# A state-space block and a mixture of experts on one core: the low parts of the expert weights move from GpSimd to VectorE

## The reference

```
x  = x + layernorm(scan(layernorm(x)))          # selective state-space scan, 16 states
xt = layernorm(x)                               # T x 512
p  = softmax(xt @ gate_w)                       # 8 experts
for k in 0, 1:                                  # the two best experts of a token
    e, w  = k-th best expert and its probability
    pos   = place of the token among those of its expert
    keep  = pos < 640
    h = gelu(xt @ w1[e] + b1[e]);  y = h @ w2[e] + b2[e] + gelu(xt @ wd[e]) @ wu[e]
    out += keep * w * y
out += 0.2 * (gelu(xt @ sw1 + sb1) @ sw2 + sb2 + gelu(xt @ swd) @ swu)     # shared expert
x  = x + layernorm(out)
```

## Time and profile before

| what | value |
|---|---|
| median of three runs | 3465.41 us (3461.23 to 3466.05) |
| profiled execution: time, span | 3467.13 us, 3465.4 us |
| granted TensorE clock, mean | 0.937 |
| busy: PE, DVE, ACT, POOL | 3129.6, 1893.0, 1418.3, 1764.3 us |
| the same as share of the span | 90%, 55%, 41%, 51% |

### The profile page before, as it was taken

The page is one execution under the profiler, slowest core; times in us unless marked ns, Lnnn a source line. Parts: engine busy times, 40 slices in busy tenths (PEclk is TensorE's granted clock), DMA queues, the critical chain, the costliest instruction groups (busy, mean ns, idle before and its releaser), DMA issues.

```text
span 3465.4 us, 42917 instructions
## 1 busy us (share of the span) xinstructions
PE 3129.6 (90%) x15139; PEld 2558.2 (74%) x15139; DVE 1893.0 (55%) x2592; ACT 1418.3 (41%) x2514; POOL 1764.3 (51%) x1655
## 2 busy tenths in 40 slices
PE   6455698989989999899999999999999999999997
PEld 3233477777767777788888888888888888888886
DVE  6698899898988994562232232232322322322456
ACT  7554576766767665321221321322312213213233
POOL 1086888888878795551441541523513414416324
PEclk8655799999999999999999999999999999999999
DMA  7859597786968865930330320412312303304355
GB/s 253 253 174 229 183 242 194 222 235 191 270 183 235 218 199 187 282 92 19 76 77 13 98 62 15 119 35 49 98 22 68 82 16 92 67 10 109 72 179 164
DMA packets 277800, 466.31 MB, mean 135 GB/s; under 512 B 31073, under 2 KB 106545, under 8 KB 277586
## 3 DMA queue, kind: packets, MB, share of 16 engines
q1 hardware_dynamic: 209104, 273.30, 27.4%
q0 software_dynamic: 66720, 189.87, 20.9%
q10 hardware_dynamic: 1762, 0.40, 0.1%
HBM read 366.33 MB, written 97.16 MB: 134 GB/s over the span
## 4 chain that ended last, share of the span: by engine, by line
PE 52%; DVE 2%; DMA 1%; issue 1%; ACTq 1%; ACT 1%; SPq 0%; POOL 0%; POOLq 0%; DVEq 0%
PE c_psH L1953 26%; PE c_psY L1997 25%; DMA out<-d_y 1%; PE c_psT L1944 1%; ACTq L48 1%; DVE hh L1685 1%; DVE yst L1669 1%; PE c_psY L1993 0%; DVE hl L1687 0%; ACT h L1415 0%; ACT h L1417 0%; PE c_psT L2052 0%; DVE hl L1680 0%; DVE wgt L1847 0%; DVE hh L1679 0%
## 5 line engine op out<-in xcount | busy, mean ns | idle before, releaser
L1685 DVE CAST hh<-h 128x512 fp32r<-128x512 f32 (+1 forms) x400 | 213.3, 533 | 1155.1 <-ACT h L1417 1148.3
L1417 ACT ACTIVATE h<-c_psH,biases 128x512 f32<-128x512 f32 (+1 forms) x400 | 248.1, 620 | 1257.4 <-PE c_psH L1953 1192.3
L837 POOL TENSOR_TENSOR u<-dtxs,Bt 128x512 f32<-128x512 f32 x512 | 669.1, 1342 | 166.4 <-DVE b_psA L739 143.9
L739 DVE TENSOR_TENSOR_SCAN b_psA<-b_psA,b_few,u 128x512 f32<-128x512 f32 x512 | 656.8, 1283 | 63.1 <-ACT b_psA L607 61.5
L1997 PE MATMUL c_psY<-W2h,hh 128*128 128x512 f32 x1344 | 540.3, 402 | 28.6 <-issue 14.7
L954 PE MATMUL b_psY<-ident,pr 128*128 128x128 f32 x2048 | 348.1, 309 | 213.4 <-DVE pr L746 195.3
L1997 PE MATMUL c_psY<-W2l,hh 128*128 128x512 f32 x1344 | 528.8, 393 | 0.0
L1997 PE MATMUL c_psY<-W2h,hl 128*128 128x512 f32 x1344 | 527.6, 393 | 0.0
L1492 POOL DMA_INDIRECT xrow<-xt_d,slot_lists x80 | 91.1, 1139 | 812.1 <-PE c_psT L1944 429.8
L954 PEld LDWEIGHTS b_psY<-ident,pr 128*128 128x128 f32 x2048 | 266.5, 157 | 298.6 <-DVE pr L746 246.4
L746 DVE TENSOR_TENSOR pr<-b_psA,Ct 128x512 f32<-128x512 f32 x512 | 354.3, 692 | 20.6 <-DMA Ct<-bc_d 3.0
(11 more groups left out here) (267 smaller groups left out, 5737.2 us busy)
## 6 DMA issues: line engine op xcount, KB each, us to landing
w<-ws_d POOLq DMA_DIRECT2D x224, 512.0 KB, 6.6
raw<-in_w SPq DMA_DIRECT2D x256, 256.0 KB, 2.7
Bt<-bc_d SPq DMA_DIRECT2D x64, 512.0 KB, 17.4
Ct<-bc_d SPq DMA_DIRECT2D x64, 512.0 KB, 19.6
xn<-in_x SPq DMA_DIRECT2D x8, 1024.0 KB, 6.3
xT_d<-xnT SPq DMA_DIRECT2D x8, 1024.0 KB, 8.4
dt_d<-a_dt SPq DMA_DIRECT2D x8, 1024.0 KB, 7.0
dtx_d<-a_dx SPq DMA_DIRECT2D x8, 1024.0 KB, 7.3
```

Source lines behind the costliest of these rows:

```text
L739: nc.vector.tensor_tensor_scan(psA[q][:, :], psA[q][:, :], u[g % U_RING][:, :], carry[:, k:k + 1], ALU.mult, ALU.add).then_inc(s_h, 1)
L837: nc.gpsimd.tensor_tensor(u[g % U_RING][:, :], dtx[s % 2][:, :], Bt[n // TG][:, n % TG, :], ALU.mult)\
L1417: nc.scalar.activation(h32[:, 0:n * P], psH[j % 2][:, 0:n * P], ACT.Gelu, bias=b1[:, j - 1:j]).then_inc(s_gelu, 1)
L1685: nc.vector.tensor_copy(hh[j % 2][a], h32[a]).then_inc(s_hhi, 1)
```

## The change

Five edits:

1. `lows` moves from GpSimd's queue to VectorE's. VectorE's `run` gets the arguments `wset` and `rest` that ScalarE's already has: in a third block, and in the shared block, it makes the low parts of chunk j - 2 after chunk j, and those of chunks 15 and 16 at chunks 1 and 3 of a first block. GpSimd keeps its DMAs alone.
2. In the shared block the one-hot rows are weighed by token number on ScalarE (64 multiplications by a per-partition scale) and no more on VectorE (8 large ones). ScalarE's extra steps come after its conversions, and the weights of the router are stored at chunk 7, not 8.
3. The logits are turned into the two PSUM banks of the row transposes (`psT`) and no more into the banks of the down products (`psY`), in two halves, one after the other. VectorE copies them out after chunk 0's hidden tile (8 copies, not 4), and TensorE's `down(0)` no more waits for that copy.
4. The biases are turned into one bank, with one semaphore step.
5. In the last block of `mix`, TensorE signals each of the four output tiles when it is done, and VectorE scales them one by one.

```diff
@@ mix @@
+        s_tile = sem("b_last_tiles")
             def shared_out(b, t):
-                dve.wait_ge(s_mm2, (b + 1) * J)
+                if b < FB - 1:
+                    dve.wait_ge(s_mm2, (b + 1) * J)
+                else:
+                    dve.wait_ge(s_tile, t + 1)
...
+                        if b == FB - 1 and j == FC and t < BT - 1:
+                            last.then_inc(s_tile, 1)
-                last.then_inc(s_mm2, 1)
+                last.then_inc(s_tile if b == FB - 1 and j == FC else s_mm2, 1)
@@ experts @@
+        def logits_out(b):
+            return psT[b % 2][:, :, :].rearrange("p a b -> p (a b)")
+        def logit_column(b):
+            return 2 * P + (b % 4 // 2 * 2 + b // 4) * BT * E
@@ scalar @@
                     if wset is not None and j >= TRAIL:
                         convert_chunk(wset, j - TRAIL, at)
                     if rest is not None and j in REST_AT:
                         convert_chunk(rest[0], J - TRAIL + REST_AT.index(j), rest[1])
+                    if extra and j in extra:
+                        for part in extra[j]:
+                            part()
...
+            def weigh_one_hots(i):
+                act.wait_ge(s_heq, i + 1)
+                for o in range(BATCH):
+                    t = i * BATCH % NT + o
+                    high = high1[:, i % 2, o, :]
+                    last = nc.scalar.mul(high, high.bitcast(F32), tok_f[:, t:t + 1])
+                last.then_inc(s_high, 1)
@@ gpsimd @@
-            for j in range(J - 6):
-                lows(1, j)
             slots_known(0)
             gathers(0, 0, range(2))
             pool.wait_ge(s_wst, K * 16)
             gather_weights(0, 0)
-            for j in range(J - 6, J - TRAIL):
-                lows(1, j)
             gathers(0, 1, range(2))
             store_shared(SB - 1)
-            for j in range(J - TRAIL, J):
-                lows(1, j)
...
                 scatter(e, 1)
-                for j in range(J - TRAIL):
-                    lows(e + 2, j)
                 gathers(e + 1, 1, range(2))
                 scatter(e, 2)
-                for j in range(J - TRAIL, J):
-                    lows(e + 2, j)
                 gathers(e + 1, 1, range(2, 4))
@@ vector @@
+            def lows(s, j):
+                for w_ in pieces_of(j):
+                    _, _, hi, lo, view = piece(SHARED_W, w_)
+                    if w_ in (2, 3):
+                        hi, view = lo, view[0:LR, :]
+                    dve.wait_ge(s_whi, first_piece(s) + w_ + 1)
+                    nc.vector.tensor_tensor(lo, view, hi.bitcast(F32), ALU.subtract).then_inc(s_wlo, 1)
-            def run(at, nxt=None, extra=None, late=None, leaves=True, front=FRONT):
+            def run(at, nxt=None, wset=None, rest=None, extra=None, late=None, leaves=True, front=FRONT):
...
+                    if wset is not None and j >= TRAIL:
+                        lows(wset, j - TRAIL)
+                    if rest is not None and j in REST_AT:
+                        lows(rest, J - TRAIL + REST_AT.index(j))
...
-                dve.wait_ge(s_heq, i + 1)
-                v.tensor_tensor(high, high.bitcast(F32), spread(tok_f[:, r], E * ST), ALU.mult).then_inc(s_high, 1)
...
-            routing = {0: [less_max], 1: [probabilities, lambda: pick(0), lambda: mark(0)],
+            routing = {0: [logits, less_max], 1: [probabilities, lambda: pick(0), lambda: mark(0)],
-            run(shared(SB - 1), nxt=(expert(0, 0), X_OF[0]), front=FRONT_0, extra=routing)
+            run(shared(SB - 1), nxt=(expert(0, 0), X_OF[0]), front=FRONT_0, wset=1, extra=routing)
@@ tensor @@
                     if j == 0:
-                        if lead:
-                            pe.wait_ge(s_lg, 4)
...
             def turn_logits():
                 pe.wait_ge(s_lin, SB * 16)
+                pe.wait_ge(s_b1, 2)
+                for half in range(2):
+                    after(pe, s_lT, half)
...
```

More of the change, by code:

```diff
@@ L1420, in run @@
                         x_hi(*nxt, front.index(j - 1))
-                    if extra and j in extra:
-                        for part in extra[j]:
-                            part()
                     if weigh and j in WEIGH_AT and WEIGH_AT.index(j) < n:
@@ L1450, in store_weights @@
                         .then_inc(s_wst, 16)
-            run(shared(SB - 1), b1T[:, E * FC:], nxt=(expert(0, 0), X_OF[0], None), front=FRONT_0, wset=1, extra={1: (exponentials,), 8: (store_weights,)})
+            def weigh_one_hots(i):
[5 more added lines that the diff above has]
+                last.then_inc(s_high, 1)
+            steps = {1: [exponentials], 7: [store_weights]}
+            for i, j in enumerate(BATCH_AT):
+                steps.setdefault(j, []).append(lambda i=i: weigh_one_hots(i))
+            run(shared(SB - 1), b1T[:, E * FC:], nxt=(expert(0, 0), X_OF[0], None), front=FRONT_0, wset=1, extra=steps)
             def expert_blocks(e, last=False):
@@ L1479, in _ @@
         def _(pool):
-            def lows(s, j):
-                for w_ in pieces_of(j):
-                    _, _, hi, lo, view = piece(SHARED_W, w_)
-                    if w_ in (2, 3):
-                        hi, view = lo, view[0:LR, :]
-                    pool.wait_ge(s_whi, first_piece(s) + w_ + 1)
-                    nc.gpsimd.tensor_tensor(lo, view, hi.bitcast(F32), ALU.subtract).then_inc(s_wlo, 1)
             def gather(e, k, t):
@@ L1916, in first_block @@
             def first_block(e):
-                run(expert(e, 0), late=expert(e - 1, 2), nxt=(expert(e, 1), X_OF[1]), extra={12: (lambda: scatter_rows(e),)})
+                run(expert(e, 0), late=expert(e - 1, 2), nxt=(expert(e, 1), X_OF[1]), rest=e + 1,
+                    extra={12: (lambda: scatter_rows(e),)})
             for e in range(E - 1):
@@ L1922, in _ @@
                 expert_slots(e + 1)
-                run(expert(e, 2), late=expert(e, 1), nxt=(expert(e + 1, 0), X_OF[0]))
+                run(expert(e, 2), late=expert(e, 1), nxt=(expert(e + 1, 0), X_OF[0]), wset=e + 2)
             e = E - 1
@@ L2018, in turn_biases @@
                 pe.wait_ge(s_bin, 32)
-                nc.tensor.transpose(psT[0][:, 0, :], raw[0][:, 0:P], ident[:, :]).then_inc(s_bt, 1)
-                nc.tensor.transpose(psT[1][:, 0, 0:FC], raw[1][0:FC, 0:P], ident[0:FC, 0:FC]).then_inc(s_bt, 1)
+                nc.tensor.transpose(psT[0][:, 0, :], raw[0][:, 0:P], ident[:, :])
+                nc.tensor.transpose(psT[0][:, 1, 0:FC], raw[1][0:FC, 0:P], ident[0:FC, 0:FC]).then_inc(s_bt, 1)
             def turn_logits():
                 pe.wait_ge(s_lin, SB * 16)
-                for t in range(NT):
-                    b = t // BT
-                    k, o = b % 4 * 32, (b // 4 * BT + t % BT) * E
-                    last = nc.tensor.transpose(psY[b % 4][:, o:o + E], logits_in(b)[:, t % BT * P:(t % BT + 1) * P],
-                                               ident[k:k + E, k:k + E])
-                last.then_inc(s_lT, 1)
+                pe.wait_ge(s_b1, 2)
+                for half in range(2):
+                    after(pe, s_lT, half)
+                    for t in range(NT):
+                        b, o = t // BT, logit_column(t // BT) + t % BT * E
+                        if b % 4 // 2 == half:
+                            k = b % 4 * 32
+                            last = nc.tensor.transpose(logits_out(b)[:, o:o + E],
+                                                       logits_in(b)[:, t % BT * P:(t % BT + 1) * P], ident[k:k + E, k:k + E])
+                    last.then_inc(s_lT, 1)
             def cumulate():
```

19 lines of the change are left out of this document (9 added, 10 removed).

## The result

The kernel after takes 3419.96 us in the median of four runs (3419.75 to 3425.09), the kernel before 3465.73 beside it; the ratio is 0.9874 [0.9857, 0.9892]. Forecast were 3419 us, within 3411 to 3434. The profiled execution took 3419.83 us, its span is 3418.1. The mean granted clock rose from 0.937 to 0.944. In a second round, where the kernel after ran again as `after_again`, it took 3427.98 us beside 3469.14, a ratio of 0.9879 [0.9863, 0.9896]: 41.2 us and not 45.8. The change is worth 41 to 46 us, and the forecast's 46.2 was met at the upper end.

The account below looks back on a forecast made before the run. GpSimd's subtractions were taken to hold VectorE's copies and so TensorE, whose clock then drops. Gains of 34.9 + 6.5 + 3.0 + 1.8 = 46.2 us off the profiled 3467.13 gave 3420.9, or 3419.2 for a median; range 3411 to 3434.

Parts of the forecast that it names:

- First blocks: First blocks of experts 1 to 7: without GpSimd's subtractions VectorE's copy is no longer held; gain 34.9 us, bounds 33.2 to 36.6.
- The 1.7 us kept for `hl` at chunk 1: First blocks: half of the remaining 3.4 us of TensorE's waits for a low part, taken as staying; bounds 0 and 3.4.
- rival B: First blocks, chunk 3: VectorE's own queue keeps the stall; 3454 us, or 3433 for a part of it; chance 0.06 together.
- Second and third blocks: Low parts on VectorE in third blocks hide behind TensorE, and second and third blocks show no loss to remove; 0 us.
- rival D: Third blocks: VectorE's queue, waiting for raw weights, becomes the bound and the kernel gets slower; chance 0.04.
- no wait: Third blocks: a sign of being right was that ScalarE no longer waits for raw weights, 28.3 us in 7 waits before.
- Shared block, late: Late stall of TensorE in the shared block: 4.15 us of wait and 2.3 of slow clock both go; 6.5 us.
- Shared block, early: Start of the shared block: earlier first down product and clock lead by 5.1 us, of which 3.0 stay; bounds 0 and 5.1.
- I take another 0.6 off: Shared block, chunks past 4: allowance for ScalarE's one-hot multiplications and a full VectorE, cutting the lead from 3.6 to 3.0 us.
- End of `mix`: Last block of mix: scaling tile by tile puts three of four output tiles ahead of the last matmul; 1.8 us, or 0.
- rival A: Shared block: the early lead is 0 and up to 10 us more go in chunks 4 to 9; 3422 to 3432; chance 0.14.
- Rival C: First blocks: VectorE's subtractions hold GpSimd's scatters, the last ending 2.8 us later, so ScalarE waits; 3439 us; chance 0.05.

Follow-up runs that it names:

- pauses: Kernel before, but GpSimd waits for its own last subtraction to end before starting the next; 3436.52 us, ratio 0.9907.
- last_four_back: Kernel after, but the four subtractions of chunks 15 and 16 return to GpSimd behind its scatters, for experts 1 to 7; 3455.83 us, ratio 0.9958.
- three_more_steps: Kernel after with shared-block chunk 0's low parts before second pick, one-hots weighed on VectorE, third scatter held until next block's chunk 0 is split; 3424.07 us.
- low_parts_longer: Kernel after with two needless statistics operations on VectorE ahead of each main-weight subtraction, from expert 1's third block on; 3433.54 us, ratio 0.9893.
- logits_back: Kernel after with the logits again turned into the down products' banks, so the first down product waits for their copy; 3421.19 us, ratio 0.9885.
- weigh_on_vector: Kernel after with the one-hot rows weighed on VectorE again, none on ScalarE; 3418.37 us, ratio 0.9874.
- low_first: Kernel after with chunk 0's low parts in the shared block made ahead of the second pick and mark; 3420.52 us, ratio 0.988.
- pairs_back: Kernel after with the last four output tiles of mix scaled only after the last matmul again; 3423.24 us, ratio 0.9889.
- two_input: Kernel before with the hidden tile's high part made as its maximum with itself, a two-input operation, instead of a copy; 3478.47 us, ratio 1.0023.
- only_lows: Kernel before with only the move of the low parts from GpSimd to VectorE; 3429.26 us, ratio 0.9885.

## Why the prediction was right

**First blocks (34.9 forecast, 34.9 measured).** `pauses` and `last_four_back` show the cause. The 1.7 us kept for `hl` at chunk 1 were right in size and not in place: the wait that stays, 0.24 us a block above expert 0's (50.08 against 49.84), is at `down(0)`, behind VectorE's small copy, which takes 0.60 us beside a scatter. In `three_more_steps` the scatter is held back, and the blocks take 49.75 to 49.78 us (one takes 50.11). The subtractions at chunks 1 and 3 of a first block cost nothing, as the count of 2.8 us of work in 2.8 said; rival B did not come.

**Second and third blocks (0 forecast, 0.6 us lost).** The third blocks have no wait of TensorE. The 0.6 is mostly one pair of blocks, expert 3's, with 185.62 us where the others take 185.15. That is above the 185.5 which the prediction named as a sign of rival D, but it is not D: the time goes in the second block, where VectorE makes no weight. Its `down(0)` comes 0.35 us late. There a scatter began just ahead of VectorE's small copies, the first of which started 0.35 us later and the second took 0.64 us. In before the copy began 0.13 us ahead of the scatter, the copies took 0.42, and the scatter 1.74 instead of 1.57. ScalarE's waits for raw weights did not go but shrank, from 28.3 us and 2.0 (W1 and W2) to 10.6 and 6.8, none over 2.0:

```profile
ACT W1h L1380 <- DMA raw<-in_w: 10.6, 8, 1.5
ACT W2h L1380 <- DMA raw<-in_w: 6.8, 7, 2.0
```

That the loads come sooner with a quicker low part was right; "no wait" was too strong. Rival D was as far off as it looked: `low_parts_longer` nearly fills VectorE and loses nothing in these blocks.

**Shared block, late (6.5 forecast, 6.5 measured).** From `down(7)` to `down(14)` TensorE leads over before by 1.6 us throughout; at the end of the block it is 8.1, and the wait of 4.15 us is gone.

**Shared block, early (3.0 forecast, 1.6 measured in this trace).** This term was mis-sized, and 1.6 is the best that it shows. At `down(14)`, ahead of the late stall, the five traces of this same block lead over before by 1.6, 1.2, -0.8, -0.8 and -1.5 us (a minus is a lag); three are below the lower bound of 0. Its first half was right in direction: `down(0)` came 2.27 us earlier (2.3), and with the clock at 1.00 the lead at `down(1)` was 4.8 (5.1), though other traces have 1.1 to 2.2 and 3.7 to 4.7; `logits_back` gives back 2.7 us of wait and the clock of 0.60.

Of this lead 3.2 us were lost again, not 2.1: 0.9 by `down(4)` (35.63 us after the stage's start before, 31.71 after), 0.6 at `down(5)` and 1.5 at `down(7)` (52.88 and 51.28). The first loss was forecast at 1.5, and with it that the raw weights of chunk 1 land no sooner was right: their last cast comes 29.19 us after the stage's start, 29.70 before.

The step "I take another 0.6 off" for the chunks after it is the one that failed: 2.3 went there. Two things make it up. ScalarE's eight multiplications of 2.13 us in all stand ahead of a gelu and cost 1.5 us at `down(7)`, as `weigh_on_vector` shows. The other losses, 0.9 by `down(4)` and 0.6 at `down(5)`, hang on chunk 1's weights, which are late: with `low_first` they are gone, and with both edits (`three_more_steps`) the whole 3.2 us are. That these two start later is not the reason, as `after_again` starts as late and loses 3.8 from `down(1)` to `down(7)`. The pace of the weights is not the cause: chunks 1 to 4 are cast over 17.6 us, and TensorE needs 17.3 for `down(4)` to `down(7)` in before. How soon the first weight could come if GpSimd's loads were not beside it, no run shows.

The five traces differ mostly by the clock (last section), besides one longer wait at chunk 4 in `last_four_back`. This is rival A in part: its waits came at chunks 4, 5 and 7, and the term fell short by 1.4 us here and by 4.5 in `after_again`.

**End of `mix` (1.8 forecast, 1.8 measured).** The timeline of VectorE:

```profile
1406.72 1.37 DVE L791 SCALAR_TENSOR_TENSOR xn<-b_psS,sb2bc 128x512 f32<-128x512 f32 x2
```

TensorE's last matmul ends at 1407.36 and this pair at 1408.09, so 0.73 us behind it; before it was 2.52. `pairs_back` gives 1.9 us back at the meeting of the engines. The other 1.1 of the 2.96 us is `mix` itself, which the change does not touch and which differs from run to run: over the traces of this study `experts` starts between 1409.6 and 1427.6 us.

**What lay outside the sum.** The 1.9 us of the table's last row above the sum came from no edit: over the traces this stretch is 201.2 to 204.3 us, in kernels with and without the change (and 205.5 in `two_input`). It makes up for the 1.4 us of the shared block, and with the 1.1 us of `mix` the sum came out closer than its terms. So the mechanism and the large terms were right, and that the median fell within 1 us of the forecast was luck: in the second round the same change gained 4.6 us less.

**Rival C** was a scatter held by VectorE's subtractions. One of four took 1.99 us and not 1.57, 0.4 us more where the rival asked for 2.8, and the waits of ScalarE have none for a scatter.

## What to carry to other kernels

A row of VectorE that is ten times its usual length tells to look at what GpSimd does in the same microseconds, and to compare the ends of the two. If a row of instructions of GpSimd can't be moved away, a wait between each two of them lets VectorE in; here that alone gave 32.6 us, with GpSimd busy 2.4 us more, where moving the work gave 41 to 46. VectorE is then still held for one instruction, which left a wait of 0.7 us in each first block. And a stall of TensorE costs more than its length through the clock (4.15 us of wait cost 6.5, 2.67 cost 3.7 to 4.8, and the same wait of 2.9 in first blocks cost 3.4 to 6.2), so sum the blocks, not the waits.

## What the runs showed of the hardware

- Subtractions of GpSimd that stand in a row leave no gap: 1.8 us long, they start 1.25 us apart beside a held copy in a first block, and 1.25 to 1.29 us long, they start as far apart in the shared block. VectorE gets no access between them, whether it copies or subtracts: 5.08 us behind four, 8.41 over six. With a wait between, each takes 1.27 to 2.15 us, and VectorE is held for one.
- VectorE makes a low part of 128x512 in 0.68 us, where GpSimd takes 1.62 in the mean for W1 and 1.39 for W2. GpSimd is busy 375 us less and VectorE 82 more; VectorE's 288 subtractions alone sum to 187, and its own held operations got shorter.
- A scatter of GpSimd and VectorE disturb each other little: a copy of 32x256 took 0.60 us beside one instead of 0.29, and a scatter beside two subtractions 1.99 instead of 1.57.
- The same kernel with the same waits can be granted a different clock. In `after_again` the shared block took 110.80 us and not 107.72. One us of this is lost by `down(0)`, 9.91 us after the stage's first matmul and not 8.95: the clock of this stretch is 0.74, and 0.83 in after. The largest part, 1.6 us, is lost between `down(7)` and `down(8)`, behind a wait of 0.68 us that after has too. There this window has a clock of 0.83, where the same window of after has 1.00. The prediction's sign, a clock of 1.00 in all windows of `experts` past its first 4 us, thus came true in after as long as TensorE works, and not in `after_again`:

```profile
1460.00:1470.00 10.00, 8.88 (x36) 7.00 (x35) 5.58 (x8) 6.91 (x22) 0.00 (x0) 0.83 1.12 342
```

So a difference of some 3 us in the shared block between two single traces, as for `only_lows`, tells little unless its waits and windows are read too.
